# Layer 3's neighbour scores of six batch pairs, spread by two DMA transfers through DRAM instead of TensorE transposes

## What is computed

```python
Wh = jnp.einsum('bnf,fo->bno', h, W)
s1 = Wh @ a1
s2 = Wh @ a2
e = s1[:, :, None] + s2[:, None, :]
e = jnp.where(e >= 0, e, ALPHA * e)
e = jnp.where(adj_matrix[None] == 0, -jnp.inf, e)
attention = jax.nn.softmax(e, axis=-1)
h_prime = jnp.einsum('bij,bjo->bio', attention, Wh)
```

## Time and profile before

| | us |
|---|---|
| median of three runs | 568.5 |
| the profiled execution | 569.67 |
| its span | 567.8 |
| PE busy | 533.0 (94%) |
| DVE busy | 419.2 (74%) |
| ACT busy | 373.9 (66%) |
| POOL busy | 198.8 (35%) |

### The profile page before, as it was taken

One profiled execution on the slowest core, in us unless ns is written; L12 is line 12 of the kernel. 1 busy time (PEld: TensorE's weight loads), 2 busy tenths in 40 slices (PEclk: granted clock), 3 DMA queues, 4 the chain that ended last, 5 costly groups with the idle time before them and its releaser, 6 DMA issues.

```text
span 567.8 us, 11229 instructions
## 1 busy us (share of the span) xinstructions
PE 533.0 (94%) x3522; PEld 464.6 (82%) x3522; DVE 419.2 (74%) x1466; ACT 373.9 (66%) x749; POOL 198.8 (35%) x240
## 2 busy tenths in 40 slices
PE   7899999797999989999999999999999999999871
PEld 5788734575887988998999999999998998989861
DVE  4588677889787644479787787788688776778887
ACT  4577594676656636256695785786787687685681
POOL 7930350337366312315226126216216116210203
PEclk9899999999999999999999999999999999999997
DMA  8222100132100000000000100100100100100012
GB/s 227 76 81 74 39 0 0 55 95 64 48 0 2 1 0 1 1 2 1 1 2 2 37 1 0 38 0 0 37 0 0 37 0 0 39 0 2 1 38 74
DMA packets 28383, 15.26 MB, mean 27 GB/s; under 512 B 2320, under 2 KB 28048, under 8 KB 28352
## 3 DMA queue, kind: packets, MB, share of 16 engines
q1 hardware_dynamic: 27792, 13.65, 8.4%
q0 software_dynamic: 560, 1.25, 0.7%
HBM read 10.69 MB, written 4.19 MB: 26 GB/s over the span
## 4 chain that ended last, share of the span: by engine, by line
PE 76%; DVE 13%; ACT 3%; issue 2%; POOL 2%; DMA 1%; SPq 1%; DVEq 0%; POOLq 0%; ACTq 0%
PE psum L291 14%; PE psum L293 14%; PE psum L292 14%; PE psum L2004 9%; PE psum L1811 5%; PE psum L1859 3%; PE psum L1946 3%; PE psum L1956 3%; PE psum L1883 2%; PE psum L1870 2%; PE psum L1874 2%; PE psum L2050 2%; PE psum L2032 2%; DVE ln_st L188 2%; DVE soft L1029 1%
## 5 line engine op out<-in xcount | busy, mean ns | idle before, releaser
L207 POOL TENSOR_TENSOR ln_r<-ln_v,mhalf 128x8 f32<-128x8 f32 x27 | 44.6, 1651 | 225.7 <-DVE ln_v L201 225.7
L2004 PE MATMUL psum<-l2w_s,h 128*128 128x128 f32 x512 | 59.8, 276 | 0.0
L2004 PEld LDWEIGHTS psum<-l2w_s,h 128*128 128x128 f32 x512 | 59.0, 192 | 0.8
L291 PE MATMUL psum<-qt_hi,l2w_s_hi 128*128 128x512 f32 x128 | 52.8, 412 | 0.0
L293 PE MATMUL psum<-qt_hi,l2w_s_lo 128*128 128x512 f32 x128 | 50.8, 396 | 0.0
L292 PE MATMUL psum<-qt_lo,l2w_s_hi 128*128 128x512 f32 x128 | 50.7, 396 | 0.0
L285 ACT ACTIVATE keep_x<-keep_x,ln_b,ln_r (+1 forms) x108 | 44.4, 487 | 8.2 <-DVE keep_x L277 5.6
L1559 ACT ACTIVATE h<-psum 128x512 f32<-128x512 f32 x60 | 34.8, 593 | 11.7 <-PE psum L293 11.6
L291 PE MATMUL psum<-wgt_hi,h_hi 128*128 128x256 f32 x128 | 37.1, 290 | 0.9 <-DVE h_lo L1006 0.9
L293 PE MATMUL psum<-wgt_hi,h_lo 128*128 128x256 f32 x128 | 35.8, 280 | 0.0
L292 PE MATMUL psum<-wgt_lo,h_hi 128*128 128x256 f32 x128 | 35.8, 279 | 0.0
(11 more groups left out here) (284 smaller groups left out, 1746.8 us busy)
## 6 DMA issues: line engine op xcount, KB each, us to landing
xin<-in_x SPq DMA_DIRECT2D x64, 128.0 KB, 2.3
out_x<-ob SPq DMA_DIRECT2D x24, 128.0 KB, 1.8
out_x<-keep_x SPq DMA_DIRECT2D x8, 128.0 KB, 1.9
l2w_raw<-in_l2w POOLq DMA_DIRECT2D x1, 512.0 KB, 5.8
adjs<-in_adj SPq DMA_DIRECT2D x1, 256.0 KB, 2.8
adjs<-in_adj_t SPq DMA_DIRECT2D x1, 256.0 KB, 3.0
l2w_s<-in_l2w POOLq DMA_DIRECT2D x1, 256.0 KB, 5.5
w_raw<-in_w_t SPq DMA_DIRECT2D x1, 128.0 KB, 3.0
```

Of the source, the lines that this page charges most:

```text
L207: pool.tensor_tensor(ln.r[:].rearrange("p s k -> p (s k)"), ln.v[:].rearrange("p s k -> p (s k)"), mhalf[:], ALU.pow).then_inc(ln.root, 1)
L291: pe.matmul(o, lhs[0], rhs[0], start=start, stop=False)
L2004: i = pe.matmul(bank(s)[:, 0, k * D:(k + 1) * D], h2[:, s, g, j * N + t * P:j * N + (t + 1) * P], l2w3_s[:, g, :], start=(g == 0), stop=(g ...
```

## The change

For iterations 0 to 5 (six iterations, twelve slots) `spread3` goes from PE's steps. In its place SP writes the four s2 columns of a slot to a DRAM tensor `s2_rows`, 512 single values of 4 bytes, waits until they have landed (`row_out`), and reads them back as one row of 512 values into all 128 partitions of `s2_bc` (`row_in[s]`). `s2_bc` takes the SBUF space of `l2w2_raw`, which is dead by then. DVE waits for both slots' `row_in` just ahead of `s3_low(p, 0)`, and `scores3` reads `s2_bc` from SBUF instead of a PSUM bank. PE's `mix_x` waits for `h2_out` instead of `tm_done`. Iterations 6 and 7 keep the transposes.

```diff
-        l2w2_raw = sb("l2w2_raw", [P, GA, H2B])
+        l2w2_raw, s2_bc = in_turn(lambda c: sb("l2w2_raw", [P, GA, H2B], scope=c), lambda c: sb("s2_bc", [P, 2, 2 * N], scope=c))
+        s2_rows = nc.dram_tensor("s2_rows", (2, 4, P), F32).ap()
@@ sync
-            with sp.Fori(0, IT - 2) as p:
+            def score_rows(p):
+
+                for s in range(2):
+                    sp.wait_ge(s12_ok, 2 * p + s + 1)
+                    sp.dma_start(s2_rows[s].rearrange("k n -> n k"), s12[:, s, 1, :],
+                                 allow_slow_non_contiguous=True).then_inc(row_out, 16)
+                    sp.wait_ge(row_out, 16 * (2 * p + s + 1))
+                    sp.dma_start(s2_bc[:, s, :], s2_rows[s].rearrange("k n -> (k n)").partition_broadcast(P)).then_inc(row_in[s], 16)
+
+            def store_sums(p):
                 for s in range(2):
 
                     sp.wait_ge(ln3.done, 2 * p + s + 1)
                     for t in range(T):
                         sp.dma_start(out_nat[:, t, bass.ds(4 * p + 2 * s, 2), :], ob[:, s, t, :, :]).then_inc(stored[s], 16)
+
+            score_rows(0)
+            with sp.Fori(1, IT - 2) as p:
+                score_rows(p)
+                store_sums(p - 1)
+            store_sums(IT - 3)
@@ vector, own_scores and scores3
-                                                         op0=ALU.mult, op1=ALU.mult, accum_out=s12[:, s, c, k:k + 1])
+                                                         op0=ALU.mult, op1=ALU.mult,
+                                                         accum_out=s12[:, s, c, (k, T * (k % 2) + k // 2)[c]].unsqueeze(1))
-                    wait_apart(dve, dc, s2_done, 2 * p + s + 1)
                     for k in range(4):
-                        i = dve.tensor_tensor_reduce(out=soft[:, s, k, :], in0=bank(4 + s)[:, 0, (k % 2) * N:(k % 2 + 1) * N],
+                        i = dve.tensor_tensor_reduce(out=soft[:, s, k, :], in0=s2_bc[:, s, (k % 2) * N:(k % 2 + 1) * N],
@@ vector, step, between ln_var_eps and s3_low(p, 0)
+                if behind:
+                    for s in range(2):
+                        dve.wait_ge(row_in[s], 16 * p)
                 s3_low(p, 0)
@@ tensor, step
                 for s in range(2):
-                    if two_behind:
-
-                        pe.wait_ge(tm_done, 2 * (p - 2) + s + 1)
-                    elif not first:
+                    if not first:
 
                         pe.wait_ge(h2_out, GB * 2 * p)
                     mix_x(p, s)
...
-                if behind:
-
-                    pe.wait_ge(h2_out, GB * (2 * p + 1) + 2)
-                    for s in range(2):
-                        spread3(p - 1, s)
```

More of the change, by code:

```diff
@@ L313, in build @@
         o2_done = sem("o2_done")
+        row_out, row_in = sem("row_out"), [sem("row_in0"), sem("row_in1")]
         s12_ok, s2_done, tm_done, m_step = sem("s12_ok"), sem("s2_done"), sem("tm_done"), sem("m_step")
@@ L1188, in end_maxima @@
             def end_maxima(s):
-                dve.wait_ge(s2_done, 2 * L + s + 1)
+                dve.wait_ge(s2_done, 2 + s + 1)
                 for k in L3_ORDER:
@@ L1262, in slot_maxima @@
             def slot_maxima(p, s):
-                dve.wait_ge(s2_done, 2 * p + s + 1)
+                dve.wait_ge(s2_done, s + 1)
                 for k in range(4):
```

## The result

The changed kernel took 646.4 us (median of 4 runs, 645.3 to 647.7) against 568.9 for the kernel before, run beside it: ratio 1.137, 95% interval 1.133 to 1.142. The forecast was 579.7 with a range up to 588. So the sign held and the size did not: +77.5 us instead of +11.2. The profiled execution has a span of 645.4 us where it was 567.8.

What follows compares the result with a forecast made beforehand. PE's stream was taken as the bound, with ACT's chain ending beside it. Step 1 +7.4 us, steps 2 to 4 +4.0, steps 5 and 6 -0.2: +11.2, giving 579.7 us as a median, range 572.5 to 588.

Steps and rivals of the forecast that it cites:

- What bounds the kernel: Around the change PE is always busy and sets the time; ACT's scalings, s_hi and s_lo end with it at mix_out(p, 1).
- Credit 0.1 us a step for the transposes: Steps 2 to 6: of 0.87 us saved on PE per step, only 0.1 reaches the end; the rest becomes waiting for s_lo.
- The transfers: Per slot, a write W taken as 3.0 us (bounds 1.8 and 5.7) and a read R as 3.0 (bounds 2.3 and 4.1).
- Steps 2 to 6. Cost nothing: Both slots' transfers land at about 397.1 in step 4, needed at 398.77: covered with 1.7 us to spare.
- 388.1 + 2W + R: Step 4's data arrival time from write landing W and read landing R; the cover ends at 2W + R = 10.7.
- Step 1: No cover there: data at 273.7 delays mix_out(1, 1) by 5.1 us; with 2.3 for the stall, 7.4 in all.
- The stall beside GpSimd: Maxima with two SBUF inputs take turns with weigh, 2.34 us longer: +1.33 a step in steps 2 to 4, +2.34 in step 1.
- Rival 1: Transfers slower than their cover in steps 2 to 6 (W about 4.5): 586 us, about 604 at both upper bounds; chance 0.14.
- Rival 2: No stall of the maxima beside POOL: 573.1 us, or 571.2 with both landings at their lower bounds; chance 0.20.
- Rival 3: Only PE's work counts, data in time in step 1 too, so the full 5.2 us is saved: 563.3 us; chance 0.03.
- Rival 4: Within 0.5%: lower-bound transfers, no stall and faster maxima from SBUF, +2.2 us, 570.7 us; chance 0.05.
- Sign: Whole kernel: slower by over 0.5% at chance 0.92, within 0.05, faster 0.03.

Runs made afterwards that it cites:

- run 7: The run 3 kernel with GpSimd's weigh moved behind its next ln_power and ScalarE's s_hi of slot 1 ahead of its last two scalings: 565.0 us, ratio 0.994.
- run 10: The kernel before, transposes kept, with only the two moves of run 7 on GpSimd and ScalarE: 567.9 us, ratio 1.001.
- run 3: The changed kernel without transfers or the wait for them, s2_bc set to zero once: 575.0 us, ratio 1.012 to the kernel before.
- run 1: The changed kernel writing 128 pieces of 16 bytes instead of 512 of 4, maxima reading with a stride: 585.7 us, ratio 1.029 to the kernel before.
- run 2: The changed kernel with DVE's wait for the rows moved behind s_lo of both slots: 636.8 us, ratio 1.120 to the kernel before.
- run 5: The changed kernel with 22 idle matmuls ahead of mix_out(p, 0) to keep TensorE busy in its wait: 645.7 us, ratio 1.135 to the kernel before.
- run 9: The changed kernel with both slots' writes issued before one wait, then both reads: 601.2 us, ratio 1.059 to the kernel before.
- run 6: The kernel before plus probe writes of five shapes and reads on SP's idle queue: 16-byte pieces 1.42 us, the change's write 8.18 in the first round.
- run 11: The kernel before plus probe writes of 128 4-byte pieces at four spacings and touching 8-byte pieces: 8 bytes apart 2.9 us, 64 apart 1.4.

## Why the prediction was wrong

- **What bounds the kernel: right.** TensorE's stream sets the time, with ACT's and DVE's chain ending beside it. Runs 7 and 10 show both for a kernel whose scores are never late. In the kernel after it is the transfers that bound six steps.
- **Credit 0.1 us a step for the transposes: right where the scores are never late.** In run 3 `s_lo` stands 43.52 us apart from step 5 to step 6, where there is no `weigh`, and stood 43.60 apart before. They give 0.87 only when the other chain is shortened (run 7). In the kernel after they give nothing, as TensorE waits where they were.
- **The transfers: the step that failed.** "Bounds for the write: 1.8 us ... and 5.7 ... I take 3.0" was mis-sized: 8.0 and 10.6 us. The lower bound was a store in rows of 512 bytes, the upper one a load, whose DRAM side is only read: neither writes pieces of 4 bytes that touch in DRAM, and the likeness in size (2 KB, 128x4) meant nothing. The estimate that the prediction works out from the Trainium skill, page DMA: Bandwidth & Descriptors, section Anatomy of one DMA, is missed as well: it has 2.0 us for the write and 2.6 for the read, where 8.0 to 10.6 and 4.9 were measured. The Trainium skill gives that sum for transfers that GpSimd issues, while these are SyncE's. R = 3.0 was right for a read alone (3.0 to 3.1) and 4.9 for read 1 in step 4.
- **"Steps 2 to 6. Cost nothing" fell with it.** The formula held: 388.1 + 2W + R with 8.0 + 10.6 for the writes and 4.9 for the read gives 411.6, 12.8 us past 398.77; the stretch of step 4 was 12.3 us longer than before. The threshold 2W + R = 10.7 fits as well, though no run lies close to it: with 1.7 and 3.7 (7.1) run 1 waits in step 1 alone.
- **Step 1.** Forecast wait some 6 us, `s_lo` 273.7; measured 284.59 with a wait of 19.0, and TensorE idle 16.1 and 2.4 us ahead of the two `mix_out`. Here the path was wrong too: the forecast counted one write and one read from slot 1's scores, but write 1 was issued only at 269.27, when write 0 had landed, 3.7 us behind those scores. So step 1 as well is slot 0's scores plus two writes and a read.
- **The stall beside GpSimd: the mechanism was right, its size and its place off.** 1.7 us instead of 2.34 for four `weigh`; 0.6 a step instead of 1.33 (run 3). Taking turns leaves a small overlap, which the forecast had at nothing. In the kernel after it shows in step 1 only (the maxima span 4.5 us for 2.8): later `weigh` is long done when DVE's wait ends. When the data is never late, step 1 has most of it, 4.3 us, as the maxima then also meet the cast and the subtraction (run 3).
- **Rivals.** Rival 1 was the one that came true, and my own bounds for it stopped at 604 (605.5 if its terms are added up again). Its condition was stated, its price was capped by rows that did not contain the shape. I gave it 0.14. Rivals 2 to 4 are refuted by run 3 and the result.
- **Sign.** Slower was right, with a sum seven times too small.

The sum by the measured terms: step 1 16.8, steps 2 to 6 59.3 (table), after them 1.5: 77.6.

## What to carry to other kernels

A transfer's price depends on how its pieces lie in DRAM and not only on their count and size: keep at least 16 bytes of each partition together in a write (1.4 us for 8.2 here), or space the pieces. Where the trace does not show a shape, the nearest row is no bound; ask what happens at several times it, and how often per step it is waited for (here twice in a row, in six steps). Here a latency longer than its cover was paid in each of six steps; a later wait got 9.6 of 77.5 us back (run 2) and a full clock at most a few (run 5), while a shorter stretch got 61 and 44 back (runs 1 and 9).

## What the runs showed of the hardware

- Writes of 4-byte pieces from 128 partitions into DRAM: 1.4 to 4.0 us with one piece in 16 bytes, 2.6 to 3.0 with two (pieces of 8 bytes that touch among them), 6.7 to 8.2 with four, with 128 pieces nearly as much as with 512. In the slow one of 512 pieces the profile shows the DMA engines idle for the last 6.9 of 8.1 us (runs 6, 11). Two such writes overlap (run 9: 8.1 us each, 3.2 us apart).
- The same read of a 2 KB row into 128 partitions: 3.0 to 3.1 us alone, 3.7 in run 1, 4.8 in the kernel after.
- The maxima read from SBUF as fast as from PSUM (0.42), with a stride of 16 bytes at 0.60 (one every 0.53 us instead of 0.34).
- With both inputs in SBUF they alternate with GpSimd's multiplications, one for one: 0.82 to 0.87 each, one every 0.76 us; beside a subtraction of 1.28 us one took 1.49 (run 3).
- TensorE's granted clock was at 0.53 in the stretch in which it came out of its wait and at 1.00 in the next; that cost 0.3 to 1.2 us a step in steps 2 to 6 (run 5).
